# Layer-2 attention: the attention core two steps further behind its feed, the value operand filled three steps later

## The reference

```python
x = x + _L2_xattn_ref(_layernorm(x, axis=-1), ctx_1024, Wq, Wkv, Wc)

qp = jnp.einsum('bld,ed->ble', q, Wq)
scores = jnp.einsum('bld,bmd->blm', qp, kv)
idx = jnp.argmax(scores, axis=-1)                       # one context row per token
mem = jnp.take_along_axis(kv, idx[..., None], axis=1)
mk, mv = jnp.split(jnp.einsum('bld,ed->ble', mem, Wkv), 2, axis=-1)   # one 8-wide head
qh = qp.reshape(b, l, 16, 8).transpose(0, 2, 1, 3)
logits = jnp.einsum('bhld,bmd->bhlm', qh, mk) * scale
out = jnp.einsum('bhlm,bmd->bhld', softmax(logits), mv)
return jnp.einsum('bld,ed->ble', out.transpose(0, 2, 1, 3).reshape(b, l, d), Wc)
```

## Time and profile before

| | |
|---|---|
| median of three runs | 3581.4 us (3580.28 to 3582.94) |
| profiled execution | 3559.48 us, span 3557.9 us |
| TensorE matmul busy | 2806.2 us, 79% |
| VectorE busy | 2226.2 us, 63% |
| ScalarE busy | 1219.6 us, 34% |
| GpSimd busy | 433.6 us, 12% |
| mean granted TensorE clock | 0.859 of full |
| layer-2 attention, first normalised row to last statistics | 1861.92 to 2308.5 us |

### The profile page before, as it was taken

One profiled execution on the slowest core, in us unless ns is written; L12 is line 12 of the kernel. 1 busy time (PEld: TensorE's weight loads), 2 busy tenths in 40 slices (PEclk: granted clock), 3 DMA queues, 4 the chain that ended last, 5 costly groups with the idle time before them and its releaser, 6 DMA issues. The chain is left out here.

```text
span 3557.9 us, 66932 instructions
## 1 busy us (share of the span) xinstructions
PE 2806.2 (79%) x24556; PEld 1846.6 (52%) x24556; DVE 2226.2 (63%) x5515; ACT 1219.6 (34%) x1872; POOL 433.6 (12%) x748
## 2 busy tenths in 40 slices
PE   5867769995999999999987888799852676885356
PEld 4623325663666666666545555466541564664126
DVE  6765548995355555555546777777014557997668
ACT  4535548883000000000016566455320113442230
POOL 0011110000000000000000000034033003442003
PEclk9955559997999999999988888899975778997568
DMA  2010000002121212121200000010322220000001
GB/s 83 27 54 1 1 10 17 15 12 96 60 84 53 91 48 95 48 95 48 95 8 16 10 9 9 2 41 27 90 65 61 60 53 3 0 0 7 0 0 47
DMA packets 88409, 136.96 MB, mean 38 GB/s; under 512 B 42949, under 2 KB 54597, under 8 KB 87242
## 3 DMA queue, kind: packets, MB, share of 16 engines
q1 hardware_dynamic: 80746, 114.75, 10.2%
q0 software_dynamic: 7520, 20.34, 1.9%
HBM read 117.75 MB, written 17.30 MB: 38 GB/s over the span
## 5 line engine op out<-in xcount | busy, mean ns | idle before, releaser
L1424 PE MATMUL banks<-l1f_xe,l1f_w 128*128 128x512 f32 x1024 | 486.7, 598 | 11.1 <-DVE l1f_xe L1623 11.1
L1623 DVE TENSOR_TENSOR l1f_xe<-l1f_hT,l1f_rwb 128x512 f32<-128x512 f32 x256 | 173.3, 692 | 301.0 <-PE banks L1426 278.2
L1426 PEld LDWEIGHTS banks<-l1f_w,l1f_xe 128*128 128x128 f32 x2048 | 269.5, 192 | 123.5 <-issue 123.5
L1629 DVE TENSOR_TENSOR l1f_ae<-l1f_aoT,l1f_rwb 128x512 f32<-128x512 f32 x256 | 172.7, 690 | 160.3 <-PE banks L1454 156.1
L1426 PE MATMUL banks<-l1f_w,l1f_xe 128*128 128x128 f32 x2048 | 270.2, 275 | 0.0
L1424 PEld LDWEIGHTS banks<-l1f_xe,l1f_w 128*128 128x128 f32 x1024 | 176.9, 192 | 141.8 <-issue 127.5
L1454 PE MATMUL banks<-l1f_ae,l1f_w 128*128 128x512 f32 x512 | 225.3, 598 | 1.4 <-DVE l1f_ae L1629 1.4
L1454 PEld LDWEIGHTS banks<-l1f_ae,l1f_w 128*128 128x128 f32 x512 | 97.1, 192 | 118.3 <-issue 116.1
L223 PE MATMUL banks<-consts,l3p_h 128*128 128x128 f32 x64 | 17.8, 433 | 164.6 <-DVE l3p_h L140 164.6
L601 PE MATMUL banks<-l0f_b,l0f_back 4*128 4x512 f32 x128 | 132.6, 1137 | 0.0
L214 POOL COPY x<-xn 128x512 f32 (+1 forms) x16 | 9.8, 610 | 972.7 <-DVE xn L1653 972.7
(11 more groups left out here) (490 smaller groups left out, 6375.5 us busy)
## 6 DMA issues: line engine op xcount, KB each, us to landing
l1f_rwb<-l1f_shares SPq DMA_DIRECT2D x128, 512.0 KB, 4.5
l3p_ctx<-in_ctxT SPq DMA_DIRECT2D x32, 256.0 KB, 3.9
l0a_ctxT<-in_ctxT SPq DMA_DIRECT2D x16, 256.0 KB, 2.7
l2f_sent<-l0f_zero SPq DMA_DIRECT2D x4, 1024.0 KB, 7.0
l1a_ctxT<-in_ctxT SPq DMA_DIRECT2D x16, 256.0 KB, 2.6
l2c_ctxT<-in_ctxT SPq DMA_DIRECT2D x16, 256.0 KB, 2.7
l2e_rows<-l2f_sent SPq DMA_DIRECT2D x16, 256.0 KB, 2.8
l2f_answers<-l2e_y POOLq DMA_DIRECT2D x16, 256.0 KB, 2.7
```

The lines of the kernel that those rows point to most:

```text
L1424: pe.matmul(bank, w[:, n, e, :], xe[:, e % NB, :], start=(e == 0), stop=(e == E - 1))
L1426: last = pe.matmul(v_bank[:, D * j:D * j + D], xe[:, e % NB, P * j:P * j + P], w[:, 2, e, :], start=(e == 0 and j == 0), stop=(e == E - 1) ...
L1623: dve.tensor_tensor(xe[:, e % NB, :], hT[:, m, :], rwb[:, m, e, :], ALU.mult).then_inc(s.xe_ready, 1)
L1629: dve.tensor_tensor(ae[:, e % NB, :], aoT[:, m, :], rwb[:, m, e, :], ALU.mult).then_inc(s.ae_ready, 1)
```

## The change

The parts of the core move from lags 12, 13, 14, 15 to 14, 15, 16, 17 on all engines (copy_mv from 16 to 18), so a tile's scores are taken two steps later with respect to the feed. The feed stays where it is, but for spread_v on VectorE, which goes from lag 10 to 13. No instruction of a tile or a group is added or taken away; the unrolled head of the program gets longer (TensorE and VectorE enter the loop at n = 32 and not 24).

```diff
@@ gpsimd
-            pipeline(pool, k.NT, [(16, lambda t, r: core.copy_mv(pool, t, r)), (9, at_group(keep_q))], unroll=RING, behind=8)
+            pipeline(pool, k.NT, [(18, lambda t, r: core.copy_mv(pool, t, r)), (9, at_group(keep_q))], unroll=RING, behind=8)
@@ tensor
-            pipeline(pe, k.NT, [(12, lambda t, r: core.score(pe, t, r)), (13, lambda t, r: core.turn(pe, t, r)),
-                                (15, lambda t, r: core.project(pe, t, r)), (14, lambda t, r: core.weigh(pe, t, r)),
+            pipeline(pe, k.NT, [(14, lambda t, r: core.score(pe, t, r)), (15, lambda t, r: core.turn(pe, t, r)),
+                                (17, lambda t, r: core.project(pe, t, r)), (16, lambda t, r: core.weigh(pe, t, r)),
                                 (3, at_group(turn)), (4, at_group(queries)), (5, at_group(choose)), (7, at_group(turn_hot)),
@@ scalar
-            pipeline(act, k.NT, [(13, lambda t, r: core.copy_pT(act, t, r)), (12, lambda t, r: core.exp(act, t, r)),
+            pipeline(act, k.NT, [(15, lambda t, r: core.copy_pT(act, t, r)), (14, lambda t, r: core.exp(act, t, r)),
@@ vector
-            pipeline(dve, k.NT, [(12, lambda t, r: core.centre(dve, t, r)), (14, lambda t, r: core.normalise(dve, t, r)),
-                                 (15, lambda t, r: core.new_x(dve, t, r)), (6, at_group(choose)), (8, at_group(store_v)),
-                                 (10, at_group(spread_v))],
+            pipeline(dve, k.NT, [(14, lambda t, r: core.centre(dve, t, r)), (16, lambda t, r: core.normalise(dve, t, r)),
+                                 (17, lambda t, r: core.new_x(dve, t, r)), (6, at_group(choose)), (8, at_group(store_v)),
+                                 (13, at_group(spread_v))],
```

## The result

The changed kernel takes 3521.06 us (median of four runs, 3516.19 to 3524.86), the kernel before, timed beside it, 3581.23 us (median of four, 3580.28 to 3582.94): ratio 0.9831, 95% interval 0.9814 to 0.9848, 60 us faster. 3520 was forecast.

The account below looks back on a forecast made before the run. Bound: VectorE's new_x, choose, spread_v and centre in steps 2 and 3 delay TensorE's score and lower its clock. Groups -66.3, start -5, end +9.8 give -61.5 us: 3581.4 to 3520 us, range 3508 to 3546.

Parts of the forecast that it names:

- Which edge bounds: Steps 2 and 3, 12.98 us: VectorE's new_x, choose, spread_v, then centre hold up TensorE's score of step 0.
- Thirteen groups: Steady groups of the attention phase: 21.66 us each, 281.6 against 347.88 us, so -66.3 us.
- Start: Start of the phase: early steps hold feed alone without scores; -5 us, ends 0 and -6.
- End: Drain of the phase: tiles finish two steps later, plus one unhidden new_x; +9.8 us, ends +7.8 and +11.7.
- Cover in steps 0 and 1: VectorE takes new_x in step 0 with 2.0 us of cover, spread_v in step 1 with 1.4 us; TensorE sees nothing.
- Slack itself worth nothing: Scores two steps further from spread_k: no score waits for ScalarE's kbd, so slack alone gains nothing and costs 0.
- From the profiled time to the runs: Whole program: profiled 3559.48 would become 3498, run median 3581.4 would become 3520 us; other phases keep their instructions.
- Part 1: new_x and spread_v leave VectorE's step 2: steps 2 and 3 take 10.19 us instead of 12.98, spread_v being 0.49.
- 2.15 us left it up: TensorE's clock stays at 1.00: longest idling 1.66 us, and an early gap of 2.15 us had not lowered it.
- Rival (a): Clock still falls in every group, step 0 takes 8.26 us, group 24.49: 3557 us; chance 0.16 with its in-between.

Follow-up runs that it names:

- extra_step2: Changed kernel with 2.15 us of unused VectorE row maxima added once a group at the end of step 2: 3587.84 us, ratio 0.9993 to the kernel before.
- extra_half_step3: Changed kernel with 0.54 us of unused VectorE work added once a group at the end of step 3: 3526.57 us, ratio 0.9835 to the kernel before.
- core1: Kernel before with the core one step later and spread_v at lag 13: 3498.58 us, ratio 0.9827 to the kernel before.
- core3: Kernel before with the core three steps later and spread_v at lag 13: 3499.04 us, ratio 0.9834 to the kernel before.
- before_again: The kernel before, unchanged, run again on chip B: 3587.01 us, ratio 0.9998 to the kernel before.
- after_again: The changed kernel, unchanged, run again on chip B: 3528.77 us, ratio 0.9825 to the kernel before.

## Why the prediction was right, point by point

- **Which edge bounds.** Right, and shown by work put back on it (extra_step2: the whole gain lost) and beside it (extra_half_step3: nothing lost, for half a microsecond).
- **Thirteen groups.** 21.66 us forecast, 280.68 / 13 = 21.59 measured; -67.2 for -66.3.
- **Start.** Forecast -5. The row maximum of step n = 16 is at 1905.74 and was at 1910.98 (5.2 earlier), but the phase itself began 2.0 us earlier (first normalised row at 1859.89 and not 1861.92), so -3.2; between before_again and after_again it is -3.2 too.
- **End.** 43.23 - 33.97 = +9.3 for +9.8. Sum -67.2 - 3.2 + 9.3 = -61.1, the -61.0 of the phase; -61.5 forecast. That it comes so near is luck in part: the end of this profile has two spells of low clock, that of after_again has none and takes 40.84 us, 5.7 more than the end of before_again.
- **Cover in steps 0 and 1.** Right: new_x starts 5.06 us after the score of step 0 (+4.75 forecast), TensorE waits nowhere in these steps, VectorE has 1.34 to 1.73 us left in step 1 (1.4 forecast). The row maximum of step 1 follows at +7.2 (+7.0 forecast) without idling before it.
- **Slack itself worth nothing.** Right: core1, core3.
- **From the profiled time to the runs.** The forecast of the profiled time (3498) was off by 26 us, because I took the rest of the program as fixed from one execution to another. The median came out since both medians were taken side by side, and the difference of the attention phases carries over.
- **What was mis-sized.** Part 1 gave spread_v 0.49 us a group, 6 us in all. Undone, it costs 30.5 us of the phase. And "2.15 us left it up" was a poor ground for the clock: it was one early gap, and 2.17 us lowers the clock in every steady group of core2_spread10. For core2_spread10, the change with spread_v left in step 2, the expectation said 3528, and its ratio of 0.9915 puts it at 3551 on the same scale. The clock stayed up because the idling came out at 1.53 to 1.71 us (1.66 forecast), just under where it begins to fall (four groups of twelve at 1.73 to 1.91). The size of that margin was not forecast; on this point, worth some 30 us in core2_spread10, the prediction was lucky.

Rival (a) was thus nearer than its 0.16: its clock fell in every group of the kernel one half microsecond away, with a step 0 of 7.0 us there and not the 8.26 that (a) took.

## What to carry to other kernels

In a hand-written step pipeline look at which parts of one engine fall on the same step modulo the group, and move one of them by any number of steps that changes this. Here one, two and three steps gave the same; more depth by itself gave nothing. Price a gap ahead of TensorE in two terms, its own length and the spell of low clock behind it, and read from steady groups of the same kernel, not from a single early gap, from which length on the second sets in. It can be a range and not a point. Subtract profiles of two kernels phase by phase before their totals: here the totals differed by 35 us, the phase by 61, the runs by 60.

## What was not expected of the hardware

Half a microsecond of idling moved the cost of a group by 2.0 us (21.6 to 23.6), through the granted clock. In two kernels with 1.7 to 1.9 us of idling and in one with 2.0 to 2.3 the groups of one execution split into two lengths some 1.6 us apart, and the same gap of 2.06 us in the same program lowered the clock in one execution and not in another. The same kernel took 3557, 3581, 3589 and 3588 us in four places, each within 0.3% of its own median; in the profiles some 30 us of such a difference lie in one phase, which takes 410 us in one place and 436 or more in another with the same instructions.
